# A conv, attention and scan kernel on one core: statistics of x through four 1 MB buffers, split arrival signals, and the second batch's first rows asked for slot by slot

## The chip, the cores and the metric

The kernel runs on one core of a Trainium2 chip. The metric is device time in microseconds (us), the median of several executions. Before the change it is 10475.02 us (three executions: 10473.13, 10475.02 and 10499.15).

## The reference, cut to what matters

```python
x = x + _L0_conv_ref(_gn(x), qkv_w, dw_w, proj_w, temperature)   # x: (2, 48, 512, 512) float32
x = x + _L1_conv_ref(_gn(x), down_w, down_b, right_w, right_b, left_w, left_b)

def _gn(v, G=16, eps=1e-5):            # group norm without scale and shift, 3 channels a group
    g = v.reshape(B_, G, C_ // G, H_, W_)
    m = jnp.mean(g, axis=(2, 3, 4), keepdims=True)
    s = jnp.var(g, axis=(2, 3, 4), keepdims=True)
    return ((g - m) / jnp.sqrt(s + eps)).reshape(v.shape)

def _L0_conv_ref(x, ...):
    qkv = conv_1x1(x, qkv_w)           # 48 -> 144 channels
    qkv = depthwise_3x3(qkv, dw_w)     # zero padding of one pixel
    q, k, v = split(qkv)               # each to (b, 8 heads, 6*16 rows, 128*128 tokens), 4x4 blocks
    q, k = q / norm(q), k / norm(k)
    attn = softmax(einsum('bhcn,bhdn->bhcd', q, k) * temperature)
    return conv_1x1(from_blocks(attn @ v), proj_w)
```

`_L1_conv_ref` runs four recurrent scans over the image (down, up, right, left), each step adding a five-tap convolution of the previous line. Only the first half of layer 0 is touched here: the group norm's mean and variance of x, and the fused 1x1 and 3x3 convolution that makes q, k and v.

## The kernel before, in words

**Stages.** `program` calls `attention`, `attention_weights_and_mix`, `scans` and `final_sum` one after the other. The change lies in `attention`, which takes the first 40% of the time. Each engine has its own instruction stream, written out by hand in the order in which it runs, and the streams meet only at semaphores.

**Statistics of batch 0.** x of batch 0 is 50.3 MB, seen as 128 partitions of 98304 numbers. SP loads it in `NCH` = 24 chunks of 2 MB (`CH` = 4096 numbers a partition) into the two slots of `xs` (`load_chunk`, L229). DVE runs eight BN_STATS of 512 numbers on each (`chunk_stats`, L528, L530), and its last one counts up `chunk_used[s]`, on which SP waits before it fills that slot again. The first two chunks are in flight before the constants and weights (`params`) are asked for; DVE then waits for `params`, multiplies the taps (L593, L595) and goes on with chunks 2 to 23. After the last chunk one aggregate (L543), two small reductions through TensorE and `row_stats` give mean and variance of every channel. Statistics of batch 1 are taken later, by small chunks, beside the convolution of batch 0; they are not touched.

**Convolution blocks.** A block is four image rows (`NT` = 128 blocks a batch). `raw` and `raw_edge` have two slots; block n lies in slot n % 2. `load_main` (L232) issues five DMAs: channels 0 to 31 in three row shifts and channels 32 to 47 in two. `load_edge` (L236) issues four: channels 32 to 47, the third row shift, in four column shifts. All nine count up one semaphore, `raw_in[b][s]`. ACT waits for all nine (`arrive`, L304), then makes `x_high` of x minus its mean (`high`, L297, k = 0 to 3, one a row) and `x_edge` (L300, k = 4 and 5). DVE makes the rounding remainder `x_low` (L629) and the lower half of `x_edge` (L633); its last one counts up `low_ready[b]`. That count tells PE that a block can be multiplied, and SP that its raw slot is free. PE computes four output rows a block (`row`, L430), each into one of two PSUM banks; ACT takes a row out (`take`, L334 and L335), DVE adds the other half to it (`add_up`, L644 and L645, signal `dve_moved`), and PE starts row dy only when row dy - 2 has been moved. ACT's order in a block is fixed: casts 0, 1, 2 of the next block, take 0, cast 3, square, cast 4, take 1, cast 5, the v copy, take 2, take 3.

**Borders.** Row -1 of the image is outside. `fill_top` (L610) writes the mean into row 0 of `raw` slot 0 and into the two border columns of `raw_edge`, of both slots at once, and signals `top_filled[b]`. `fill_end` (L619) does the same for the last row.

**The change of batch.** In before, SP loads blocks 0 and 1 of batch 1 when `top_filled[1]` has come. DVE runs `fill_top(1)` behind its `add_up` calls of block 126, after `low_ready[0]` = 128. ACT meets the wait for block 0 of batch 1 (`arrive(1, 0, 0)`) at the start of its block 127, ahead of its four takes of block 127. At the start of batch 0 SP asks for the main rows of blocks 0 and 1 early, and for the edge rows only after `top_filled[0]`.

Of the kernel before, what the change touches and what calls it, by code (L numbers as in the profile page):

```python
# [16 lines left out]
B, C, H, W = 2, 48, 512, 512  # L17
# [75 lines left out]
def attention(nc, sem, x, wqkv, dwqkv, gstat, gsel, g112, ident, weights, eye, g112_sb, sumsq, ones, gram_sb,  # L93
# [6 lines left out]
    EDGE = 64  # L100
    CH, FM = 4096, 512
    NCH = C * H * W // 128 // CH
# [10 lines left out]
    with ExitStack() as inner:  # L113
            def sbi(name, shape, dt=F32):
                return inner.enter_context(nc.sbuf_tensor(name, shape, dt))
# [9 lines left out]
            scan_taps = sbi("scan_taps", [PP, len(weights), 3, PP])  # L125
            xs = sbi("xs", [128, 2, CH])
            stats = sbi("stats", [128, NCH * PER, 6])
# [11 lines left out]
            vt = sbi("vt", [TOK, 2, HEADS, N * N, HC])  # L139
            v_out = xs[0:HD, 0, 0:2 * HEADS * (NB // 2) * TOK].rearrange("p (f h i t) -> p f h i t", f=2, h=HEADS, t=TOK)  # L140
            qk = xs[:, 1, 0:2 * HQ * HD].rearrange("p (s h n c) -> p s h n c", s=2, h=HQ, c=HC)
            xs1 = sbi("xs1", [128, 2, SMALL])
# [8 lines left out]
            cleared, params = sem("cleared"), sem("params")  # L151
            chunk = [sem("chunk0"), sem("chunk1")]
            chunk_used = [sem("chunk_used0"), sem("chunk_used1")]
            small = [sem("small_chunk0"), sem("small_chunk1")]
# [8 lines left out]
            def per_batch(name):  # L163
                return [sem(f"{name}_b{b}") for b in range(B)]

            raw_in = [[sem(f"qk_raw_in_b{b}_{s}") for s in range(2)] for b in range(B)]
            top_filled, end_filled = per_batch("top_filled"), per_batch("end_filled")
            high_ready, low_ready = per_batch("high_ready"), per_batch("low_ready")
# [3 lines left out]
            v_stored = [[sem(f"v_stored_b{b}_{s}") for s in range(2)] for b in range(B)]  # L172
            LOADS = 9

# [28 lines left out]
            with nc.Block() as block:  # L203
# [17 lines left out]
                def _(sp):  # L221
# [10 lines left out]
                    def load_main(b, n, s, top=False, end=False):  # L232
                        for at, ch, nch, shift in ((0, 0, 32, -1), (32, 0, 32, 0), (64, 0, 32, 1), (96, 32, 16, -1), (112, 32, 16, 0)):
                            to, frm = rows(n, shift, top, end)
                            sp.dma_start(raw[at:at + nch, s, to], x[b, ch:ch + nch, frm]).then_inc(raw_in[b][s], 16)
                    def load_edge(b, n, s, end=False):  # L236
                        to, frm = rows(n, 1, False, end)
                        for k in range(4):
                            a, e = max(0, 1 - k), min(W, W + 1 - k)
                            sp.dma_start(raw_edge[16 * k:16 * k + 16, s, to, a:e],  # L240
                                         x[b, 32:C, frm, a - 1 + k:e - 1 + k]).then_inc(raw_in[b][s], 16)

# [3 lines left out]

                    for s in range(2):
                        load_chunk(s, s)
# [10 lines left out]
                    for half in range(2):  # L259
                        for k in range(4):  # L260
                            at = 64 * half + 16 * k
                            sp.dma_start(w1[at:at + 16, 1], wqkv[32:C]).then_inc(params, 16)
                            for d in range(2):
                                if 0 <= d - k + 2 < 3:
                                    sp.dma_start(dwe[at:at + 16, d],
                                                 dwqkv[2, d - k + 2].unsqueeze(0).broadcast_to([16, QKV])).then_inc(params, 16)
                    with sp.Fori(1, NCH // 2) as i:
                        for s in range(2):

                            sp.wait_ge(chunk_used[s], i)  # L270
                            load_chunk(2 * i + s, s)
                    sp.wait_ge(tiles_clear, 1)
                    load_main(0, 0, 0, top=True)
                    load_main(0, 1, 1)
                    for b in range(B):
                        sp.wait_ge(top_filled[b], 1)
                        if b:
                            load(b, 0, 0, top=True)
                            load(b, 1, 1)
                        else:  # L280
                            load_edge(b, 0, 0)
                            load_edge(b, 1, 1)
                        with sp.Fori(1, NT // 2 - 1) as i:
                            for s in range(2):

                                sp.wait_ge(low_ready[b], 2 * i + s - 1)
                                load(b, 2 * i + s, s)
                        for s in range(2):
                            sp.wait_ge(low_ready[b], NT - 3 + s)
                            load(b, NT - 2 + s, s, end=s == 1)  # L290

                @block.scalar
                def _(act):
# [10 lines left out]
                    def arrive(b, n, s):  # L304

                        act.wait_ge(raw_in[b][s], 8 * LOADS * (n - s) + 16 * LOADS)

# [29 lines left out]
                    def group(b, g, first=False, last=False):  # L337
                        for i in range(NB):
                            n = NB * g + i
                            s = (i + 1) % 2  # L340
                            to_b, to_n = b, n + 1
                            if last and i == NB - 1:
                                to_b, to_n = b + 1, 0

                            def casts(*ks):
                                if to_b < B:
                                    for k in ks:
                                        high(to_b, to_n, s, k)

                            if to_b < B:  # L350
                                if last and i == NB - 2:
                                    act.wait_ge(end_filled[b], 1)
                                if last and i == NB - 1:
                                    act.wait_ge(negmean_ready, to_b + 1)

                                if not (first and i == 0):
                                    act.wait_ge(conv_done[b], N * n)
                                arrive(to_b, to_n, s)
                            casts(0, 1, 2)
                            if not (first and i < 2):  # L360

                                act.wait_ge(gram_done[b], n - 1)
                                act.wait_ge(vt_done[b], n - 1)
                            take(b, n, i, 0)
                            casts(3)
                            if not (first and i == 0):
                                square(b, n - 1, i - 1, first and i == 1)
                            casts(4)
                            take(b, n, i, 1)
                            casts(5)  # L370
                            if not (first and i == 0):
                                v_block(b, n - 1, g if i else g - 1, (i - 1) % NB)
                            take(b, n, i, 2)
                            take(b, n, i, 3)
# [18 lines left out]
                    arrive(0, 0, 0)  # L393
                    for k in range(CASTS):
                        high(0, 0, 0, k)
# [124 lines left out]
                def _(v):  # L520
# [66 lines left out]
                    nc.vector.memset(sumsq[:], 0.0).then_inc(sums_clear, 1)  # L587
                    for s in range(2):
                        v.wait_ge(chunk[s], 16)
                        chunk_stats(s, s)  # L590
# [5 lines left out]
                    link(ins)  # L596
                    with v.Fori(1, NCH // 2) as i:
                        for s in range(2):

                            v.wait_ge(chunk[s], 16 * i + 16)  # L600
                            chunk_stats(2 * i + s, s)
                    for s in range(2):
                        v.wait_ge(chunk_used[s], NCH // 2)
                    own_means()
# [4 lines left out]

                    def fill_top(b):  # L610

                        for a, e in ((0, 32), (96, 112)):
                            nc.vector.tensor_copy(raw[a:e, 0, 0], mean0[a:e, 0, b:b + 1].broadcast_to([e - a, W]))
                        for at in (0, W - 2):
                            ins = nc.vector.tensor_copy(raw_edge[:, :, :, at:at + 1].rearrange("p s r one -> p (s r one)"),
                                                        mean0[0:EDGE, 1, b:b + 1].broadcast_to([EDGE, 2 * N]))
                        ins.then_inc(top_filled[b], 1)

# [37 lines left out]
                    def group(b, g, first=False, last=False, sampled=False):  # L656
                        for i in range(NB):
# [23 lines left out]
                            if last and i == NB - 3:  # L681
                                v.wait_ge(low_ready[b], NT - 2)
                                fill_end(b)
                            if last and i == NB - 2 and b + 1 < B:
                                v.wait_ge(low_ready[b], NT)
                                fill_top(b + 1)

                    fill_top(0)
                    scaled_taps(0)
# [916 lines left out]
```

## Time and profile before

| What | Value |
|---|---|
| Median of three executions | 10475.02 us |
| Profiled execution: span, first to last instruction | 10449.6 us |
| Median less span (launch and end, outside the span) | 25.4 us |
| PE, DVE, ACT busy share of the span | 90%, 77%, 61% |
| Statistics of batch 0, chunks 2 to 23 | 32.44 to 167.65 us |
| First convolution of batch 0 | 191.39 us |
| PE's longest idle time between the batches | 10.07 us, until 2117.20 us |

The profile gives no time of its own for the profiled execution beyond its span, so a difference of spans is taken as a difference of times, with 25.4 us around the span. A timeline line has start, length, engine, line, operation and output <- inputs, with the count of merged instructions; the brackets at its end hold the idle time of the engine before it and what ended it. Starts are in us from the start of the span. SPq and ACTq lines are DMA issues.

### The profile page before, as it was taken

The page shows a single profiled execution, that of the slowest core. Times are in us where ns is not written, and L with a number is a line of the kernel's source. Part 1 is how long each engine was busy: PE and PEld are TensorE (multiplying, and loading weights), DVE is VectorE, ACT ScalarE, POOL GpSimd, SP SyncE. Part 2 cuts the span into 40 slices and gives each one's busy share as a digit, 9 for nine tenths or more (in the row PEclk, how much of TensorE's full clock was granted, in tenths as well). Part 3 has the DMA queues.
Part 4 walks back from the last instruction along what each step waited for, and adds up shares of the span by engine and source line. Part 5 has one row for each costly group of instructions (what it writes and reads, how often), then busy time and mean ns, then how long its engine had stood idle before and what let it go on. Part 6 is the DMA issues. An engine that isn't in the chain of part 4 may idle for free. (4 is left out here: it accounts for less than half of the span.)

```text
span 10449.6 us, 213663 instructions
## 1 busy us (share of the span) xinstructions
PE 9389.1 (90%) x72744; PEld 9047.4 (87%) x72744; DVE 8070.5 (77%) x16201; ACT 6339.0 (61%) x11047; POOL 2982.2 (29%) x4333
## 2 busy tenths in 40 slices
PE   2999999999999998999979999999999999999100
PEld 2999999999999998777779999999999999999100
DVE  7888888777777776998977777777799997777333
ACT  2777777767777775444456667999833336666100
POOL 0000000000000000000046666666666666666100
PEclk9999999999999998999989999999999999999555
DMA  8888887666666666999968887777766657777899
GB/s 246 166 167 164 167 166 144 125 125 130 133 129 133 132 131 127 270 266 256 267 156 198 199 202 185 211 217 214 208 209 213 220 194 190 198 197 204 346 431 406
DMA packets 740412, 2101.28 MB, mean 201 GB/s; under 512 B 58480, under 2 KB 633232, under 8 KB 649184
## 3 DMA queue, kind: packets, MB, share of 16 engines
q1 hardware_dynamic: 611920, 1744.17, 65.5%
q10 hardware_dynamic: 106368, 204.76, 6.1%
q0 software_dynamic: 22016, 151.01, 5.9%
q8 instruction: 55, 0.90, 0.0%
q14 instruction: 53, 0.43, 0.0%
HBM read 1344.51 MB, written 754.97 MB: 201 GB/s over the span
## 5 line engine op out<-in xcount | busy, mean ns | idle before, releaser
L1448 ACT CAST hi<-rough 112x256 fp32r<-112x256 f32 x4096 | 1666.8, 407 | 1410.8 <-DVE rough L1362 1359.8
L1282 PE MATMUL scan_ps<-hi,scan_high 112*112 112x256 f32 x12264 | 2125.0, 282 | 30.6 <-ACT hi L1448 30.6
L1362 DVE SCALAR_TENSOR_TENSOR rough<-scan_ps,scan_bias,lines 112x256 f32<-112x256 f32 x4086 | 2136.3, 523 | 19.0 <-issue 14.4
L1293 PE MATMUL scan_ps_low<-lo,scan_high 112*112 112x256 f32 x12264 | 2130.5, 282 | 1.1 <-POOL lo L1394 0.7
L1288 PE MATMUL scan_ps_low<-hi,scan_low 112*112 112x256 f32 x12264 | 2123.3, 281 | 0.0
L438 PE MATMUL conv_ps<-tap_high,x_high 128*128 128x432 f32 (+2 forms) x6144 | 1884.0, 307 | 27.6 <-DVE vt L645 15.7
L438 PE MATMUL conv_ps<-tap_low,x_high 128*128 128x432 f32 (+2 forms) x6144 | 1908.3, 311 | 0.0
L438 PE MATMUL conv_ps<-tap_high,x_low 128*128 128x432 f32 (+2 forms) x6144 | 1905.1, 310 | 0.0
L1282 PEld LDWEIGHTS scan_ps<-hi,scan_high 112*112 112x112 f32 x12264 | 1691.3, 175 | 32.1 <-ACT hi L1448 31.3
L1293 PEld LDWEIGHTS scan_ps_low<-lo,scan_high 112*112 112x112 f32 x12264 | 1684.7, 175 | 5.6 <-POOL lo L1394 2.8
L1288 PEld LDWEIGHTS scan_ps_low<-hi,scan_low 112*112 112x112 f32 x12264 | 1687.1, 176 | 0.0
L1394 POOL TENSOR_TENSOR lo<-lines,hi 112x256 fp32r<-112x256 f32 x2048 | 1414.5, 691 | 807.9 <-DVE lines L1367 786.2
L1394 POOL TENSOR_TENSOR lo<-ring,hi 112x256 fp32r<-112x256 f32 x2048 | 1414.0, 690 | 778.4 <-DVE ring L1367 776.7
L629 DVE SCALAR_TENSOR_TENSOR x_low<-raw,negmean,x_high 128x512 fp32r<-128x512 f32 x1024 | 1149.4, 1151 | 107.1 <-ACT x_high L297 107.1
L1367 DVE TENSOR_TENSOR ring<-scan_ps_low,rough 112x256 f32<-112x256 f32 x2044 | 868.8, 425 | 470.4 <-PE scan_ps_low L1293 436.3
L297 ACT ACTIVATE x_high<-raw,negmean 128x512 fp32r<-128x512 f32 x1024 | 1207.8, 1231 | 32.0 <-DMA raw_edge<-x 20.7
L438 PEld LDWEIGHTS conv_ps<-tap_high,x_high 128*128 128x128 f32 x6144 | 1162.1, 189 | 50.4 <-DVE vt L645 17.2
L438 PEld LDWEIGHTS conv_ps<-tap_high,x_low 128*128 128x128 f32 x6144 | 1166.4, 190 | 20.2
L438 PEld LDWEIGHTS conv_ps<-tap_low,x_high 128*128 128x128 f32 x6144 | 1162.5, 189 | 19.5 <-issue 0.2
L1367 DVE TENSOR_TENSOR lines<-scan_ps_low,rough 112x256 f32<-112x256 f32 x2044 | 867.6, 424 | 304.5 <-PE scan_ps_low L1293 222.0
L334 ACT COPY xs<-conv_ps 128x288 f32<-128x288 f32 x1024 | 408.9, 399 | 973.7 <-PE conv_ps L444 972.4
L644 DVE TENSOR_TENSOR xs<-conv_ps,xs 128x192 f32<-128x192 f32 x1024 | 365.2, 357 | 703.1 <-ACT vt L335 694.8
(140 smaller groups left out, 12398.8 us busy)
## 6 DMA issues: line engine op xcount, KB each, us to landing
raw<-x SPq DMA_DIRECT2D x764, 256.0 KB, 5.3
d_rows<-lines SPq DMA_DIRECT2D x32, 3584.0 KB, 30.2
u_cols<-lines SPq DMA_DIRECT2D x64, 1792.0 KB, 13.3
r_cols<-lines SPq DMA_DIRECT2D x32, 3584.0 KB, 24.3
lines<-u_cols SPq DMA_DIRECT2D x31, 3584.0 KB, 16.5
lines<-r_cols SPq DMA_DIRECT2D x30, 3584.0 KB, 16.6
lines<-d_rows SPq DMA_DIRECT2D x30, 3360.0 KB, 15.6
v_blocks<-xs ACTq DMA_DIRECT2D x128, 768.0 KB, 5.6
```

Source lines behind the costliest of these rows:

```text
L297: ins = nc.scalar.activation(x_high[:, s, k, :, 1:TOK + 1], phases(raw, s, k), ACT.Identity, bias=negmean0[:, 0, b:b + 1], scale=1.0)
L334: nc.scalar.copy(qk_at(i % 2, dy, 0, 3), qk_of(left))
L438: nc.tensor.matmul(bank(dy, side, lo - side, hi - side), xs[at], ws[taps], start=fresh[side], stop=False, skip_group_check=True)
L629: ins = nc.vector.scalar_tensor_tensor(x_low[:, s, k, :, 1:TOK + 1], phases(raw, s, k), negmean0[:, 0, b:b + 1], x_high[:, s, k, :, 1:TOK ...
L644: nc.vector.tensor_tensor(to(i % 2, dy, 1, 3), of(middle), to(i % 2, dy, 1, 3), ALU.add)
L1282: last = nc.tensor.matmul(ps[:, b, 0:LP], high[:, shift], hi[:, b, (k - 1) % 2, shift:shift + LP], start=shift == 0, stop=shift == 2)
L1288: nc.tensor.matmul(ps_low[:, b, 0:LP], low[:, shift], hi[:, b, (k - 1) % 2, shift:shift + LP], start=shift == 0, stop=False)
L1293: last = nc.tensor.matmul(ps_low[:, b, 0:LP], high[:, shift], lo[:, b, shift:shift + LP], start=False, stop=shift == 2)
L1362: nc.vector.scalar_tensor_tensor(rough[:, b, k % 2], ps[:, b, 0:LP], bias, line(way, s, k % T, b, kept), ALU.add, ALU.add).then_inc(rough_ ...
L1367: nc.vector.tensor_tensor(state(way, s, k, b), ps_low[:, b, 0:LP], rough[:, b, k % 2], ALU.add).then_inc(state_done[b], 1)
L1394: nc.gpsimd.tensor_tensor(lo[:, b, 1:LP + 1], state(way, k // T, k, b), hi[:, b, k % 2, 1:LP + 1], ALU.subtract).then_inc(lo_ready[b], 1)
L1448: nc.scalar.copy(hi[:, b, k % 2, 1:LP + 1], rough[:, b, k % 2]).then_inc(hi_ready[b], 1)
```

## The change

The chunk of the statistics becomes half as long and gets four slots instead of two; the loops on SP and DVE run over four slots. `v_out` and `qk`, which reuse the memory of `xs`, keep their addresses. The nine loads of a block count up two semaphores, `main_in` (5) and `edge_in` (4): `arrive` waits for the main rows alone, and ACT waits for the edge rows just ahead of cast 4. `fill_top` is called for each slot with a signal of its own. At the change of batch SP asks for the main rows of batch 1's block s as soon as `low_ready[0]` is 127 + s, and for its edge rows after `top_filled[1][s]`.

```diff
-    CH, FM = 4096, 512
+    CH, FM = 2048, 512
+    SLOTS = 4
...
-            xs = sbi("xs", [128, 2, CH])
+            xs = sbi("xs", [128, SLOTS, CH])
...
-                            sp.dma_start(raw[at:at + nch, s, to], x[b, ch:ch + nch, frm]).then_inc(raw_in[b][s], 16)
+                            sp.dma_start(raw[at:at + nch, s, to], x[b, ch:ch + nch, frm]).then_inc(main_in[b][s], 16)
...
-                                         x[b, 32:C, frm, a - 1 + k:e - 1 + k]).then_inc(raw_in[b][s], 16)
+                                         x[b, 32:C, frm, a - 1 + k:e - 1 + k]).then_inc(edge_in[b][s], 16)
...
-                    with sp.Fori(1, NCH // 2) as i:
-                        for s in range(2):
+                    with sp.Fori(1, NCH // SLOTS) as i:
+                        for s in range(SLOTS):
 
                             sp.wait_ge(chunk_used[s], i)
-                            load_chunk(2 * i + s, s)
+                            load_chunk(SLOTS * i + s, s)
                     sp.wait_ge(tiles_clear, 1)
                     load_main(0, 0, 0, top=True)
                     load_main(0, 1, 1)
                     for b in range(B):
-                        sp.wait_ge(top_filled[b], 1)
-                        if b:
-                            load(b, 0, 0, top=True)
-                            load(b, 1, 1)
-                        else:
-                            load_edge(b, 0, 0)
-                            load_edge(b, 1, 1)
+                        for s in range(2):
+                            if b:
+                                sp.wait_ge(low_ready[b - 1], NT - 1 + s)
+                                load_main(b, s, s, top=s == 0)
+                            sp.wait_ge(top_filled[b][s], 1)
+                            load_edge(b, s, s)
...
-                        act.wait_ge(raw_in[b][s], 8 * LOADS * (n - s) + 16 * LOADS)
+                        act.wait_ge(main_in[b][s], 8 * MAIN * (n - s) + 16 * MAIN)
+
+                    def edges_arrive(b, n, s):
+
+                        act.wait_ge(edge_in[b][s], 8 * EDGES * (n - s) + 16 * EDGES)
...
                                 if last and i == NB - 1:
                                     act.wait_ge(negmean_ready, to_b + 1)
+                                    act.wait_ge(top_filled[to_b][0], 1)
...
                                 square(b, n - 1, i - 1, first and i == 1)
+                            if to_b < B:
+                                edges_arrive(to_b, to_n, s)
                             casts(4)
...
                             if last and i == NB - 3:
                                 v.wait_ge(low_ready[b], NT - 2)
                                 fill_end(b)
+                                if b + 1 < B:
+                                    v.wait_ge(low_ready[b], NT - 1)
+                                    fill_top(b + 1, 0)
                             if last and i == NB - 2 and b + 1 < B:
                                 v.wait_ge(low_ready[b], NT)
-                                fill_top(b + 1)
+                                fill_top(b + 1, 1)
```

DVE's loop over the chunks and ACT's first block change in the same way: four slots in the one, and in the other casts 0 to 3 after the main rows and `top_filled[0][0]`, casts 4 and 5 after the edge rows.

SP's issues at the change of batch, before (`raw` is what `load_main` fills, `raw_edge` what `load_edge` fills):

```order
L240 DMA raw_edge<-x 16x3x510
L235 DMA raw<-x 32x1536 [waits top_filled_b1]
L235 DMA raw<-x 32x2048 x2
L235 DMA raw<-x 16x1536
L235 DMA raw<-x 16x2048
L240 DMA raw_edge<-x 16x4x511
L240 DMA raw_edge<-x 16x2048
```

The same place after:

```order
L242 DMA raw_edge<-x 16x3x510
L237 DMA raw<-x 32x1536 [waits low_ready_b0]
L237 DMA raw<-x 32x2048 x2
L237 DMA raw<-x 16x1536
L237 DMA raw<-x 16x2048
L242 DMA raw_edge<-x 16x4x511 [waits top_filled_b1_0]
L242 DMA raw_edge<-x 16x2048
L242 DMA raw_edge<-x 16x4x511
L242 DMA raw_edge<-x 16x4x510
L237 DMA raw<-x 32x2048 [waits low_ready_b0]
```

The five main DMAs of batch 1's block 0 hang on `low_ready` now, no longer on the filled border, and a wait stands ahead of its edge DMAs alone.

ACT's first block of batch 0, before:

```order
L297 ACTIVATE x_high<-raw,negmean0 128x4x128 [waits qk_raw_in_b0_0,negmean_ready,tiles_clear]
L297 ACTIVATE x_high<-raw,negmean0 128x4x128 x3
L300 ACTIVATE x_edge<-raw_edge,negmean0 64x512 x2
L297 ACTIVATE x_high<-raw,negmean0 128x4x128 [waits qk_raw_in_b0_1]
L297 ACTIVATE x_high<-raw,negmean0 128x4x128 x2
```

And after:

```order
L298 ACTIVATE x_high<-raw,negmean0 128x4x128 [waits raw_in_b0_0,top_filled_b0_0,negmean_ready,tiles_clear]
L298 ACTIVATE x_high<-raw,negmean0 128x4x128 x3
L301 ACTIVATE x_edge<-raw_edge,negmean0 64x512 [waits raw_edge_in_b0_0]
L301 ACTIVATE x_edge<-raw_edge,negmean0 64x512
L298 ACTIVATE x_high<-raw,negmean0 128x4x128 [waits raw_in_b0_1]
```

The wait for the edge rows has moved behind the four casts of the main rows.

## Rows read from the trace of the kernel before

**Rows 1.** Page: the span.
```profile
span 10449.6 us, 213663 instructions
```

**Rows 2.** Windows: busy us (count) of PE, PEld, DVE, ACT, POOL; clock, DMA, GB/s.
```profile
32.40:168.00 135.60, 0.00 (x0) 0.00 (x0) 106.80 (x177) 0.00 (x0) 0.00 (x0) 1.00 0.87 329
...
300.00:2000.00 1700.00, 1697.83 (x12693) 1670.08 (x12692) 1407.79 (x2802) 1269.08 (x1815) 48.02 (x91) 1.00 0.79 159
...
2000.00:2120.00 120.00, 109.61 (x805) 107.18 (x804) 85.61 (x180) 79.53 (x114) 0.00 (x0) 0.96 0.61 116
```

**Rows 3.** Waits from 0 to 320 us: total us, times, longest.
```profile
DVE stats L530 <- DMA xs<-x: 35.2, 23, 3.3
```

**Rows 4.** Timeline of DVE in the statistics.
```profile
32.44 4.84 DVE L530 BATCH_NORM_STATS2 stats<-xs 128x512 f32 x8 [3.26 <-DMA xs<-x]
...
37.59 4.85 DVE L530 BATCH_NORM_STATS2 stats<-xs 128x512 f32 x8 [0.31 <-DMA xs<-x]
...
45.58 9.72 DVE L530 BATCH_NORM_STATS2 stats<-xs 128x512 f32 x16 [3.15 <-DMA xs<-x]
...
107.61 4.84 DVE L530 BATCH_NORM_STATS2 stats<-xs 128x512 f32 x8 [2.31 <-DMA xs<-x]
...
162.81 4.84 DVE L530 BATCH_NORM_STATS2 stats<-xs 128x512 f32 x8 [0.93 <-DMA xs<-x]
```

**Rows 5.** DMA issues from 30 to 165 us: count, KB, us to landing.
```profile
xs<-x SPq DMA_DIRECT2D x20, 2048.0 KB, 7.2
```

**Rows 6.** Window in which both queued chunks are carried.
```profile
28.00:34.00 6.00, 0.00 (x0) 0.00 (x0) 2.74 (x8) 0.00 (x0) 0.00 (x0) 1.00 1.02 430
```

**Rows 7.** Timeline from the last statistics to the first matmul.
```profile
177.29 3.60 SPq L240 DMA_DIRECT2D raw_edge<-x  x8
...
180.08 0.45 DVE L574 TENSOR_TENSOR edge_low<-edge_f,edge_high 128x288 fp32r<-128x288 f32 x1
...
183.42 4.48 ACT L297 ACTIVATE x_high<-raw,negmean 128x512 fp32r<-128x512 f32 x4 [7.33 <-DMA raw_edge<-x]
...
187.81 2.29 ACT L300 ACTIVATE x_edge<-raw_edge,negmean 64x512 fp32r<-64x512 f32 x2
...
189.09 2.14 DVE L633 SCALAR_TENSOR_TENSOR x_edge<-raw_edge,negmean,x_edge 64x512 fp32r<-64x512 f32 x2
...
191.39 0.70 PE L438 MATMUL conv_ps<-tap_high,x_high 128*128 128x432 f32 x1 [11.96 <-DVE x_edge L633]
```

**Rows 8.** Timeline at the change of batch.
```profile
2078.44 2.19 DVE L633 SCALAR_TENSOR_TENSOR x_edge<-raw_edge,negmean,x_edge 64x512 fp32r<-64x512 f32 x2
...
2086.97 2.29 DVE L629 SCALAR_TENSOR_TENSOR x_low<-raw,negmean,x_high 128x512 fp32r<-128x512 f32 x2 [1.28 <-ACT x_high L297]
...
2098.55 0.41 ACT L334 COPY xs<-conv_ps 128x288 f32<-128x288 f32 x1 [1.54 <-PE conv_ps L444]
...
2100.74 0.24 DVE L615 COPY raw_edge<-mean 64x8 f32<-64x8 f32 x2
...
2101.01 2.17 SPq L235 DMA_DIRECT2D raw<-x  x5
...
2112.47 3.38 ACT L297 ACTIVATE x_high<-raw,negmean 128x512 fp32r<-128x512 f32 x3 [13.33 <-DMA raw_edge<-x]
...
2117.20 0.73 PE L438 MATMUL conv_ps<-tap_high,x_high 128*128 128x432 f32 x1 [10.07 <-DVE vt L645]
...
2125.66 0.40 ACT L334 COPY xs<-conv_ps 128x288 f32<-128x288 f32 x1 [2.62 <-PE conv_ps L444]
```

**Rows 9.** Page, DMA issues: count, KB, median us to landing.
```profile
raw<-x SPq DMA_DIRECT2D x764, 256.0 KB, 5.3
```

**Rows 10.** Window: the first conv row behind PE's idle time.
```profile
2117.20:2121.40 4.20, 4.20 (x16) 4.05 (x17) 4.20 (x6) 4.20 (x6) 0.00 (x0) 0.53 0.69 85
```

**Rows 11.** Timeline of ACT: take 1 of two usual blocks.
```profile
2031.47 0.41 ACT L334 COPY xs<-conv_ps 128x288 f32<-128x288 f32 x1 [0.58 <-PE conv_ps L444]
...
2046.43 0.40 ACT L334 COPY xs<-conv_ps 128x288 f32<-128x288 f32 x1 [0.56 <-PE conv_ps L444]
```

More of the change, by code:

```diff
@@ L139, in attention @@
             vt = sbi("vt", [TOK, 2, HEADS, N * N, HC])
-            v_out = xs[0:HD, 0, 0:2 * HEADS * (NB // 2) * TOK].rearrange("p (f h i t) -> p f h i t", f=2, h=HEADS, t=TOK)
-            qk = xs[:, 1, 0:2 * HQ * HD].rearrange("p (s h n c) -> p s h n c", s=2, h=HQ, c=HC)
+            v_out = flat(xs[0:HD])[:, 0:2 * HEADS * (NB // 2) * TOK].rearrange("p (f h i t) -> p f h i t", f=2, h=HEADS, t=TOK)
+            qk = flat(xs[:])[:, 2 * CH:2 * CH + 2 * HQ * HD].rearrange("p (s h n c) -> p s h n c", s=2, h=HQ, c=HC)
             xs1 = sbi("xs1", [128, 2, SMALL])
@@ L151, in attention @@
             cleared, params = sem("cleared"), sem("params")
-            chunk = [sem("chunk0"), sem("chunk1")]
-            chunk_used = [sem("chunk_used0"), sem("chunk_used1")]
+            chunk = [sem(f"chunk{s}") for s in range(SLOTS)]
+            chunk_used = [sem(f"chunk_used{s}") for s in range(SLOTS)]
             small = [sem("small_chunk0"), sem("small_chunk1")]
@@ L164, in per_batch @@
                 return [sem(f"{name}_b{b}") for b in range(B)]
-            raw_in = [[sem(f"qk_raw_in_b{b}_{s}") for s in range(2)] for b in range(B)]
-            top_filled, end_filled = per_batch("top_filled"), per_batch("end_filled")
+            main_in = [[sem(f"raw_in_b{b}_{s}") for s in range(2)] for b in range(B)]
+            edge_in = [[sem(f"raw_edge_in_b{b}_{s}") for s in range(2)] for b in range(B)]
+            top_filled, end_filled = [[sem(f"top_filled_b{b}_{s}") for s in range(2)] for b in range(B)], per_batch("end_filled")
             high_ready, low_ready = per_batch("high_ready"), per_batch("low_ready")
@@ L172, in attention @@
             v_stored = [[sem(f"v_stored_b{b}_{s}") for s in range(2)] for b in range(B)]
-            LOADS = 9
+            MAIN, EDGES = 5, 4
             def bank(dy, side, lo, hi):
@@ L266, in _ @@
                                                  dwqkv[2, d - k + 2].unsqueeze(0).broadcast_to([16, QKV])).then_inc(params, 16)
-                    with sp.Fori(1, NCH // 2) as i:
-                        for s in range(2):
+                    with sp.Fori(1, NCH // SLOTS) as i:
+                        for s in range(SLOTS):
                             sp.wait_ge(chunk_used[s], i)
-                            load_chunk(2 * i + s, s)
+                            load_chunk(SLOTS * i + s, s)
                     sp.wait_ge(tiles_clear, 1)
@@ L393, in _ @@
                     arrive(0, 0, 0)
-                    for k in range(CASTS):
+                    act.wait_ge(top_filled[0][0], 1)
+                    for k in range(N):
+                        high(0, 0, 0, k)
+                    edges_arrive(0, 0, 0)
+                    for k in range(N, CASTS):
                         high(0, 0, 0, k)
@@ L587, in _ @@
                     nc.vector.memset(sumsq[:], 0.0).then_inc(sums_clear, 1)
-                    for s in range(2):
+                    for s in range(SLOTS):
                         v.wait_ge(chunk[s], 16)
@@ L596, in _ @@
                     link(ins)
-                    with v.Fori(1, NCH // 2) as i:
-                        for s in range(2):
+                    with v.Fori(1, NCH // SLOTS) as i:
+                        for s in range(SLOTS):
                             v.wait_ge(chunk[s], 16 * i + 16)
-                            chunk_stats(2 * i + s, s)
-                    for s in range(2):
-                        v.wait_ge(chunk_used[s], NCH // 2)
+                            chunk_stats(SLOTS * i + s, s)
+                    for s in range(SLOTS):
+                        v.wait_ge(chunk_used[s], NCH // SLOTS)
                     own_means()
@@ L608, in _, with fill_top @@
                     v.wait_ge(tiles_clear, 1)
-                    def fill_top(b):
-                        for a, e in ((0, 32), (96, 112)):
-                            nc.vector.tensor_copy(raw[a:e, 0, 0], mean0[a:e, 0, b:b + 1].broadcast_to([e - a, W]))
+                    def fill_top(b, s):
+                        if s == 0:
+                            for a, e in ((0, 32), (96, 112)):
+                                nc.vector.tensor_copy(raw[a:e, 0, 0], mean0[a:e, 0, b:b + 1].broadcast_to([e - a, W]))
                         for at in (0, W - 2):
-                            ins = nc.vector.tensor_copy(raw_edge[:, :, :, at:at + 1].rearrange("p s r one -> p (s r one)"),
-                                                        mean0[0:EDGE, 1, b:b + 1].broadcast_to([EDGE, 2 * N]))
-                        ins.then_inc(top_filled[b], 1)
+                            ins = nc.vector.tensor_copy(raw_edge[:, s, :, at:at + 1].rearrange("p r one -> p (r one)"),
+                                                        mean0[0:EDGE, 1, b:b + 1].broadcast_to([EDGE, N]))
+                        ins.then_inc(top_filled[b][s], 1)
                     def fill_end(b):
@@ L683, in group @@
                                 fill_end(b)
+                                if b + 1 < B:
+                                    v.wait_ge(low_ready[b], NT - 1)
+                                    fill_top(b + 1, 0)
                             if last and i == NB - 2 and b + 1 < B:
                                 v.wait_ge(low_ready[b], NT)
-                                fill_top(b + 1)
-                    fill_top(0)
+                                fill_top(b + 1, 1)
+                    for s in range(2):
+                        fill_top(0, s)
                     scaled_taps(0)
```

## The prediction

> **What bounds the kernel now.** I read the page first: the span is 10449.6 us [rows 1], and the last chain runs through stages that the change doesn't touch, so what is gained in the attention stage shifts everything behind it. Next came the windows. In the convolution of batch 0 PE is busy 1697.8 of 1700 us [rows 2]: nothing that spares ACT or DVE a wait there can pay. Two stretches are different. In the statistics (32.4 to 168 us) PE does nothing, DVE is busy 106.8 of 135.6 us and the DMA engines 0.87 at 329 GB/s: neither is full [rows 2]. Around the change of batch PE is idle for about 10 us of 120 [rows 2]. The waits and the timelines then say what is waited for: chunks of x, 35.2 us in 23 waits [rows 3], and once at the start of each batch the edge rows, 7.33 and 13.33 us on ACT [rows 7, 8].
>
> **Term 1, statistics.** Now two slots of 2 MB alternate. DVE needs 4.84 us for eight BN_STATS (9.72 for sixteen in a row, so a change of chunk costs almost nothing) [rows 4]; a chunk takes 7.2 us from issue to landing [rows 5]; a slot's cycle is 4.84 + 7.2 + about 0.3 for signals = 12.3 us for two chunks, 6.15 a chunk. Twenty-two chunks give 135.3 us; the trace has 32.44 to 162.81 + 4.84 = 167.65, which is 135.2 [rows 4]. So it is latency that bounds, not rate.
>
> How fast does x come when a second chunk is already queued? The loop's first two chunks were: the second could start 37.59 - 32.44 = 5.15 us after the first, with DVE waiting 0.31 us for it [rows 4]. So 2 MB cost 5.15 us in a queue, against 7.2 alone, and some 2.1 us of the latency overlaps. While both are carried the engines move 430 GB/s, 4.88 us for 2 MB [rows 6]. Half a chunk then costs 2.42 us on DVE and 2.44 to 2.58 us on the DMA side. A 1 MB slot's cycle is 2.42 + 0.3 + (7.2 - 2.5) = 7.4 us, and four slots have 4 x 2.5 = 10 us for it: the queue never runs dry. I take 2.5 us a chunk, between DVE's rate and the queued DMA's. The loop's first 1 MB lands half a chunk (about 2.45 us) before 32.44, so at 30.0; two more issues ahead of the weights may delay those by up to 0.9 us, of which I take 0.4. The end is 30.4 + 43 x 2.5 + 2.42 = 140.3 us, not 167.65: **27 us gained**. Bounds: at DVE's pace 30.0 + 44 x 2.42 = 136.5, 31 us gained; at 2.58 us a chunk with the whole delay 144.3, 23 us gained. What no row shows is 1 MB pieces in this pattern, 8 KB a partition where now it is 16. Its lower bound is no gain at all, if half the bytes take half of today's pace, 3.07 us; the nearest row (two queued chunks) speaks for the upper part.
>
> The Trainium skill, "DMA: Bandwidth & Descriptors", section Bandwidth, lists 341 GB/s for one transfer of 1 MB and 425 for 16 MB; by the first a chunk would take 3.07 us, the loop 135.3 us, and this term would be nothing. The queued pair and the 430 GB/s window of this trace [rows 4, 6] stand against it, though both are of 2 MB pieces. The same section gives about 358 GB/s as what one core gets from memory; by that figure the loop's 46.1 MB need 129 us and the term is 6 us, but the trace exceeds it already.
>
> **Term 2, first block of batch 0.** The border is filled and SP issues the edge DMAs from 177.29; ACT starts at 183.42, when slot 0's have landed, and the main rows lie there long before [rows 7]. After, ACT casts rows 0 to 3 from 177.3 to 181.8 (4.48 us) and the edges from 183.4 to 185.7 (2.29 us) [rows 7]. DVE ends the scaled taps at 180.53, does four `x_low` at 1.1 us each to about 185.1, then the two edge parts in 2.14 us to 187.3, where now it ends at 189.09 + 2.14 = 191.23 [rows 7]. PE starts at 187.5, not 191.39: **4 us gained**. What is late next is DVE, not a load. Bounds 3 and 5 us. The four small copies in place of two cost DVE about 0.3 us, inside its wait.
>
> **Term 3, change of batch.** The remaining lows of block 126 end at 2078.44 + 2.19 = 2080.63 [rows 8]; that is `low_ready` = 127, so the main rows of batch 1's block 0 are issued then and not at 2101.01 [rows 8]. Five issues take 2.2 us [rows 8] and landing 5.3 [rows 9]: there by 2089. `fill_top(1, 0)` runs behind `fill_end`, ahead of the low at 2086.97. Its copies (0.84 + 0.24 us) fit the 1.28 us that DVE waits there [rows 8]. The four edge DMAs go out at 2087 and, with some 7 us as at the start, are there by 2096. ACT comes to its casts at 2098.55 + 0.6 = 2099.1 [rows 8] and waits for nothing, where now it waits 13.33 us [rows 8]. Behind those casts stand ACT's takes of block 127, which free the PSUM banks for which PE waits 10.07 us [rows 8]. PE's first row behind it runs at a granted clock of 0.53, near the lower level of 1.2 GHz, after those 10 us idle [rows 10]; that goes too. The whole of it shows in take 3 of block 127: it comes 2125.66 - 2098.55 = 27.11 us after that of block 126 [rows 8], where a usual block takes 2046.43 - 2031.47 = 14.96 us [rows 11]. **12 us gained**; bounds 10 (PE's wait alone) and 13.3 (ACT's whole wait). What is late next is the store of v and the 7 us behind it, which shift as they are.
>
> **What it adds.** Each block gets one more wait on ACT, ahead of cast 4, with a register operation in the loops. Behind it stand cast 4 and take 1, for which DVE and PE wait. In a usual block ACT waits 0.56 to 0.58 us for PE ahead of take 1 [rows 11], so an added 0.05 to 0.1 us lies in that gap: 0. Without the cover, 254 blocks at 0.1 us would be 25 us. The edge rows are asked for a block earlier and are there. The doubled number of chunk issues on SP (0.33 us each in 2.5) is no bound. PE's stream is the same.
>
> **Sum.** 27 + 4 + 12 = 43 us off the profiled execution: span 10449.6 to 10407. That execution's time outside its span is taken as the 25.4 us by which the median exceeds it, so the forecast is 10475 - 43 = **10432 us**, 0.41% less. A measurement of this kernel tells about 0.3%, 31 us, from no change: below 10444 counts as faster.
>
> **Rivals.**
> - A: the chunks keep today's pace, 3.07 us a MB, since smaller pieces don't stream at the queued pair's rate. For it: no row shows 1 MB pieces; DMA share 0.87 [rows 2] looks near full. Against: the queued pair's 5.15 us and 430 GB/s. The terms left are 4 + 12 = 16: 10459 us, no change. The row for 1 MB in the Trainium skill ("DMA: Bandwidth & Descriptors", Bandwidth) would give this case.
> - B: the wait at the change of batch moves, not goes: ACT stops for something else ahead of the takes (the early main rows behind other traffic, or the border of slot 0, late because its low is late). For: nothing in the rows is that late, the margin is 3 us at the edge rows. Against: 10 us of margin for the main rows. Term 3 gone, 31 left: 10444 us, on the boundary.
> - C, slower: transfers of one queue don't overlap their fixed part. A 1 MB chunk would then need 7.2 - 2.5 = 4.7 us, whatever is queued, 44 of them 207 us against 135: 72 us lost, 16 won, 10531 us. The case is worse than before from 3.07 + 16/44 = 3.43 us a chunk. Against it speaks again the pair 5.15 us apart where one alone takes 7.2.
>
> **Chances.** Forecast 0.77, its own range 10424 to 10442; A and what lies between (2.7 to 3.07 us a chunk) 0.13; B 0.06; C 0.04. Faster than by 0.3%: 0.77 + 0.03 from B = 0.80; within: 0.13 + 0.03 = 0.16; slower: 0.04. The range goes from 10423 (all terms at their upper bounds, 31 + 5 + 13 = 49 us, with 3 us for spread between runs) to 10455, which leaves out C and the full form of A.
>
> **What would show it.** Statistics ending near 140 us, DVE's waits there under 10 us in all, chunks every 2.4 to 2.6 us; spacings of 3 us mean A, 4.7 mean C. The first matmul of the convolution 4 us closer to the last statistics (19.7 us behind it now 23.7). At the change of batch no wait of ACT for `raw_edge`, no 10 us gap of PE, and take 3 of block 127 near 15 us behind that of 126. PE idle for more than 3 us in a middle window of 1700 us would make my zero for the added waits wrong.

## The result, and the profile after

The changed kernel takes 10425.74 us (median of 10 executions, 10405.43 to 10445.3) against 10474.69 us (10 executions, 10449.32 to 10499.15). The medians are 49 us apart. The ratio with its 95% interval, 0.9959 (0.9949 to 0.9969), stands for 43 us (32 to 53). The forecast was 43 us less and a time of 10432 us. Two later timings on other occasions, told below, gave 0.9977 for the same kernel and 0.999 for the kernel before against itself, whose two medians were 15.5 us apart all the same (10459.18 and 10474.72), so the total is known less well than one interval says. The profiled span falls by only 15.6 us, from 10449.6 to 10434.0, where the forecast had 10407. One execution of the kernel before, on a later occasion, took 18417.67 us at a granted clock of 0.551, where all others show 0.955 to 0.958; it is in none of the ratios. Where the time went is read from the traces.

Statistics, timeline of DVE after; answers to [rows 4]:

```profile
29.83 106.88 DVE L542 BATCH_NORM_STATS2 stats<-xs 128x512 f32 x172 [1.01 <-DMA xs<-x]
138.38 2.47 DVE L542 BATCH_NORM_STATS2 stats<-xs 128x512 f32 x4 [1.66 <-DMA xs<-x]
140.98 5.36 DVE L555 BATCH_NORM_AGGREGATE mv<-stats 128x2 f32<-128x1152 f32 x1
```

Its wait for chunks from 0 to 320 us (total, times, longest) and the DMA queue from 30 to 130 us, answers to [rows 3, 5]:

```profile
DVE stats L542 <- DMA xs<-x: 3.4, 4, 1.7
```

```profile
DMA packets 5777, 42.03 MB, mean 420 GB/s; under 512 B 647, under 2 KB 647, under 8 KB 647
...
xs<-x SPq DMA_DIRECT2D x40, 1024.0 KB, 7.1
```

The last statistics end at 140.85 us, not 167.65. DVE is fed without a wait for 172 instructions, which are 43 pieces in 106.88 us, 2.49 us each. A 1 MB chunk now takes 7.1 us to land, as much as 2 MB did: it stands in a queue, and that costs nothing.

First block of batch 0, timelines of SP, ACT and PE; answers to [rows 7]:

```profile
150.50 4.18 SPq L242 DMA_DIRECT2D raw_edge<-x  x8
...
150.59 4.52 ACT L298 ACTIVATE x_high<-raw,negmean 128x512 fp32r<-128x512 f32 x4 [1.28 <-DVE raw_edge L628]
156.62 2.29 ACT L301 ACTIVATE x_edge<-raw_edge,negmean 64x512 fp32r<-64x512 f32 x2 [1.51 <-DMA raw_edge<-x]
...
160.31 0.70 PE L450 MATMUL conv_ps<-tap_high,x_high 128*128 128x432 f32 x1 [7.34 <-DVE x_edge L646]
```

ACT casts while the edge rows travel; 1.51 us of waiting remain of 7.33. From the last statistics to the first matmul are 19.46 us, before 23.74.

Change of batch, timelines of DVE, SP and ACT; answers to [rows 8]:

```profile
2046.68 2.19 DVE L646 SCALAR_TENSOR_TENSOR x_edge<-raw_edge,negmean,x_edge 64x512 fp32r<-64x512 f32 x2
...
2048.90 2.18 SPq L237 DMA_DIRECT2D raw<-x  x5
...
2054.70 0.24 DVE L628 COPY raw_edge<-mean 64x4 f32<-64x4 f32 x2
...
2054.96 1.73 SPq L242 DMA_DIRECT2D raw_edge<-x  x4
...
2066.79 0.41 ACT L339 COPY xs<-conv_ps 128x288 f32<-128x288 f32 x1 [1.52 <-PE conv_ps L456]
2067.26 3.45 ACT L298 ACTIVATE x_high<-raw,negmean 128x512 fp32r<-128x512 f32 x3
...
2081.80 0.40 ACT L339 COPY xs<-conv_ps 128x288 f32<-128x288 f32 x1 [2.63 <-PE conv_ps L456]
```

The main rows go out when the low of block 126 is done, the edge rows when the border is filled, and the cast at 2067.26 has no wait. Take 3 of block 127 comes 15.01 us after that of block 126; before it was 27.11 [rows 8].

In between nothing changed; window of the changed kernel, columns as in [rows 2]:

```profile
300.00:1969.00 1669.00, 1666.81 (x12457) 1639.54 (x12455) 1380.71 (x2748) 1246.33 (x1780) 47.17 (x89) 1.00 0.78 159
```

PE idles 2.2 us in 1669, as before in 1700. The added wait in each block is hidden.

### The profile page after: what moved, and what is told of

Its sections match the earlier page's. It is cut to its first block and busy times, and to the rows that moved or that the text cites. A ratio compares the mean times of both kernels' runs of the same rounds, so it can differ in the third digit from the quotient of the medians.

```text
span 10434.0 us, 213912 instructions
## 1 busy us (share of the span) xinstructions
PE 9405.2 (90%) x72744; PEld 9056.3 (87%) x72744; DVE 8073.5 (77%) x16205; ACT 6337.2 (61%) x11047; POOL 2991.9 (29%) x4333
```

## The experiments

Four landmarks were read from every profile, in us: the start of the aggregate behind the statistics (end of statistics), the first conv matmul, the start of the last transposes of v (end of the attention stage), and the length of the mixing stage, from its first matmul to the first matmul of the scans.

| Kernel | Statistics end | First conv | Last v transposes | Mixing stage | Span |
|---|---|---|---|---|---|
| before | 167.8 | 191.4 | 4056.6 | 1207.7 | 10449.6 |
| before_again | 168.2 | 191.7 | 4052.8 | 1218.1 | 10454.0 |
| before_third | 168.0 | 191.6 | 4054.6 | 1221.7 | 10458.8 |
| after | 141.0 | 160.3 | 4009.2 | 1229.7 | 10434.0 |
| after_again | 141.3 | 160.6 | 4008.1 | 1234.7 | 10434.9 |
| stats_only | 141.6 | 165.1 | 4028.9 | 1231.9 | 10460.5 |
| signals_only | 168.3 | 187.7 | 4034.8 | 1222.5 | 10455.5 |
| handover_only | 168.8 | 192.1 | 4039.8 | 1234.8 | 10461.2 |
| split_only | 168.0 | 187.3 | 4047.5 | 1235.7 | 10462.2 |
| two_of_1mb | 198.7 | 218.0 | 4066.4 | 1212.5 | 10471.4 |
| three_of_1mb | 142.6 | 162.3 | 4009.3 | 1225.3 | 10425.1 |
| six_of_half_mb | 144.3 | 163.6 | 4011.9 | 1237.2 | 10435.2 |
| half_the_stats | 141.7 | 161.1 | 4010.1 | 1220.7 | 10424.2 |
| store_wait_later | 141.3 | 160.7 | 4006.5 | 1225.3 | 10421.2 |

### One part at a time

**stats_only**, on the kernel before:

```diff
-    CH, FM = 4096, 512
+    CH, FM = 2048, 512
+    SLOTS = 4
...
```

> The kernel before with the statistics of x through four 1 MB buffers alone; signals and the change of batch as before. Theory (three independent terms, 27 + 4 + 12 us): statistics end at 140 to 142 us as in the changed kernel, the last transposes of v in the attention stage (4056.6 us before, 4009.2 after) near 4029, total about 27 us less (10448 us). Rival (the early signals need the faster statistics, or the terms overlap): statistics end the same, but the last transposes come near 4020 or 4040.

Measured: ratio 0.9975 (0.9960 to 0.9989), which is 26 us (12 to 42). Last transposes at 4028.9, 25.8 us ahead of the mean of the three profiles of before, 4054.7. Those three spread over 3.8 us, so a distance at this landmark is good to some 2 us.

**signals_only**, on the changed kernel:

```diff
-    CH, FM = 2048, 512
-    SLOTS = 4
+    CH, FM = 4096, 512
+    SLOTS = 2
...
```

> The changed kernel with the old statistics (two buffers of 2 MB): split signals and slot-by-slot loads at the change of batch alone. Theory: statistics end at 167.6 us as before, first convolution 4 us sooner, 12 to 16 us less at the change of batch, last transposes of v near 4037, total 16 to 20 us less (10457 us). Rival (split signals cost ACT something in each of 254 blocks): last transposes near 4045 or later.

Measured: last transposes at 4034.8, 19.9 us ahead, a little better than expected. 25.8 + 19.9 = 45.7, and the whole change has 46.0 (4054.7 less 4008.7, the mean of its two profiles): at this landmark the parts add up. The totals do not: the ratio is 0.9968 (0.9956 to 0.9980), 33 us (21 to 46) where 16 to 20 were expected, and 26 + 33 = 59 us is more than the whole change gave in either timing (43 and 24 us).

**handover_only**, on the kernel before (signals of the nine loads not split; `fill_top` slot by slot as in the change):

```diff
...
-                        sp.wait_ge(top_filled[b], 1)
+                        for s in range(2):
+                            if b:
+                                sp.wait_ge(low_ready[b - 1], NT - 1 + s)
+                                load_main(b, s, s, top=s == 0)
+                            sp.wait_ge(top_filled[b][s], 1)
+                            load_edge(b, s, s)
...
```

> The kernel before with the slot-by-slot loads at the change of batch alone; one signal for all nine loads, old statistics. Theory (at the change of batch the early issue does it all, since the edge rows too are there in time): no wait of ACT at the change of batch, 12 to 16 us gained there, first block as before (ACT waits 7.3 us), last transposes of v near 4042. Rival (the split is needed there too): ACT still waits some us for edge rows, last transposes near 4048.

Measured: last transposes 14.9 us ahead of before. ACT at the change of batch:

```profile
2099.66 3.46 ACT L296 ACTIVATE x_high<-raw,negmean 128x512 fp32r<-128x512 f32 x3
```

The cast follows with no wait: there the split gives nothing.

**split_only**, signals_only with the loads at the change of batch asked for as before (DVE fills the borders of both slots behind block 126 again):

```diff
...
-                                sp.wait_ge(low_ready[b - 1], NT - 1 + s)
-                                load_main(b, s, s, top=s == 0)
-                            sp.wait_ge(top_filled[b][s], 1)
-                            load_edge(b, s, s)
+                            sp.wait_ge(top_filled[b][s], 1)
+                        for s in range(2):
+                            if b:
+                                load_main(b, s, s, top=s == 0)
+                            load_edge(b, s, s)
...
```

> The changed kernel with split signals alone: old statistics, and at the change of batch all loads are asked for only after both borders are filled, as before. Theory: first block 4 us sooner; at the change of batch ACT starts when the main rows have landed, near 4 us sooner than with all nine loads, so its wait falls from 13.3 to about 9 us; last transposes of v near 4048. Rival (split gives all of the gain at the change of batch): ACT's wait there is gone, last transposes near 4040.

Measured: last transposes 7.2 us ahead, some 4.3 of them at the first block, and ACT's wait at the change of batch:

```profile
2104.73 3.39 ACT L298 ACTIVATE x_high<-raw,negmean 128x512 fp32r<-128x512 f32 x3 [9.90 <-DMA raw<-x]
```

The wait is 9.90 us instead of 13.33, and now for main rows. Both expectations held.

### What sets the pace of the statistics

These four start from the changed kernel. **two_of_1mb** (the memory of `xs` stays as large):

```diff
-    SLOTS = 4
+    SLOTS = 2
...
```

> The changed kernel with only two of its four 1 MB buffers in use. Theory (latency: issue to landing of 1 MB is 4.7 us, of which 2.3 don't shrink with the size; slot cycle 2.45 + 0.3 + 4.7 = 7.4 us for two pieces): 3.7 us a piece, statistics end near 192 us. Rival (the gain comes from smaller pieces, not from more in flight): statistics end near 141 us or at most at 168.

Measured: statistics end at 198.7 us, 7 us later than expected. Two slots of 1 MB lose 31 us against two of 2 MB, so smaller pieces by themselves are not the gain. Its DMA issues from 32 to 130 us, and the beginning and end of one slot's cycle on DVE:

```profile
xs<-x SPq DMA_DIRECT2D x26, 1024.0 KB, 4.8
```

```profile
124.32 2.47 DVE L542 BATCH_NORM_STATS2 stats<-xs 128x512 f32 x4 [2.05 <-DMA xs<-x]
...
131.90 2.47 DVE L542 BATCH_NORM_STATS2 stats<-xs 128x512 f32 x4 [2.12 <-DMA xs<-x]
```

A slot's cycle is 131.90 - 124.32 = 7.58 us for two pieces, 3.79 each. 1 MB takes 4.8 us to land where 2 MB took 7.2 [rows 5]: by these two rows 2.4 us a MB and 2.4 us that don't shrink.

**three_of_1mb** (SLOTS = 3):

> The changed kernel with three of its four 1 MB buffers in use. Theory: slot cycle 7.4 us against 3 x 2.45 = 7.35 us of work, so just enough: statistics end at 141 to 146 us. Rival (four are needed, because a queued piece takes longer to land than one alone): 150 us or more.

Measured: 142.6 us, 1.6 us later than with four. The cycle of 7.58 us over the loads' 2.49 us a piece (below) is 3.0 slots, and three are nearly enough; the theory held.

**six_of_half_mb** (SLOTS = 6, CH = 1024):

> The changed kernel with six buffers of 0.5 MB for the statistics. Theory (with enough in flight the size of a piece does not matter, DVE's rate bounds): slot cycle 1.2 + 0.3 + 3.5 = 5 us against 6 x 1.24 = 7.4: statistics end at 140 to 142 us. Rival (a price for each piece, on the DMA side or in semaphores): 0.1 us or more a piece of 96 pieces, end at 150 us or later.

Measured: 144.3 us, between theory and rival: 3.3 us more than with four of 1 MB, which is 0.07 us for each of the 48 pieces that there are more. The core's DMA engines moved 409 GB/s from 32 to 130 us, with four of 1 MB 420; whether that or something on DVE makes the price was not separated.

**half_the_stats** (BN_STATS on every second 512 numbers):

```diff
-                        for k in range(PER):
+                        for k in range(0, PER, 2):
...
```

> The changed kernel that leaves out every second BN_STATS of the statistics of batch 0, so its means and variances are not those of x. All loads are as they were; it shows the rate of the loads alone. Theory (DVE and DMA are nearly balanced; DMA gives 430 GB/s, 2.44 us a MB): statistics end near 138 us, DVE now waiting for every piece. Rival (DMA has much in reserve, DVE alone bounds): end at 125 us or sooner.

Measured: 141.7 us, 3.7 us later than the theory had it and no sooner than with all the work. DVE's timeline:

```profile
127.34 1.29 DVE L542 BATCH_NORM_STATS2 stats<-xs 128x512 f32 x2 [1.18 <-DMA xs<-x]
...
132.31 1.29 DVE L542 BATCH_NORM_STATS2 stats<-xs 128x512 f32 x2 [1.18 <-DMA xs<-x]
```

With DVE idle half of the time the chunks still come 2.49 us apart (two spacings are 132.31 - 127.34 us), 1.049 MB / 2.49 us = 421 GB/s. The loads set the pace, and DVE, which needs 9.72 / 4 = 2.43 us a piece [rows 4], just keeps up. By this run a faster DVE would gain nothing here.

### The stages behind

> The changed kernel once more, unaltered. Theory (the attention stage is the same from run to run, the stages behind it scatter by some 20 us): last transposes of v at 4009 within 2 us, its distance to the end of the span anywhere from 6390 to 6430 us. Rival (the change costs 30 us in the stages behind): that distance is again near 6425 us, where before it was 6393, and the total ratio is nearer to 0.998.

Measured: ratio 0.9977 (0.9966 to 0.9988), 24 us (13 to 36). Last transposes at 4008.1, as the theory said; the rest of the span 6426.8 us, 6424.8 in the first profile of after and 6393.0 in that of before, as the rival said.

> The kernel before once more, unaltered, timed against itself. Theory (the stage that mixes the values scatters from execution to execution, whatever the attention stage did): last transposes of v at 4056.6 within 2 us, and the stage from there to the first scan matmul longer than in the first profile of before (1207.7 us from its first matmul), somewhere up to 1237 as in the other kernels' profiles; ratio to itself within 0.998 to 1.002. Rival (an attention stage that is over sooner makes the mixing stage 15 to 25 us longer): the mixing stage is again at 1205 to 1212 us.

> The same kernel for one more profile. Theory: its mixing stage differs by 5 us or more from one of the other two profiles of this kernel. Rival: all three lie within 5 us around 1208 us.

Measured: ratio of the kernel to itself 0.999 (0.998 to 1.000), as expected. Last transposes at 4052.8, 3.8 us before the first profile, where 2 us were allowed: a miss. The mixing stage takes 1218.1 and 1221.7 us, after 1207.7 in the first profile. So the first profile of before was one of the shorter ones, and the rival falls in the form in which it was put. But all three lie below both of after (1229.7 and 1234.7). The other nine kernels, none of which touches that stage, range from 1212.5 to 1237.2.

The same holds of the whole rest of the span, from the last transposes to its end: 6393.0, 6401.2 and 6404.2 us in the three profiles of before, 6424.8 and 6426.8 in the two of after, 6405.0 to 6431.6 in the nine others. The means of before and after differ by 26 us, 16 of them in the mixing stage and 10 in the scans. In the mixing stage the difference goes with DVE's wait for the loads of x there (`res`): 21.9, 42.9 and 42.6 us in the three profiles of before, 49.9 and 54.7 in the two of after, 31.7 in two_of_1mb, whose stage is the shortest of the nine (1212.5), and 56.6 in six_of_half_mb, whose stage is the longest (1237.2). Why those loads come later is not known. Nor is it shown that the change does it: there are few profiles, and single executions differ by as much. The first profiled execution of before, if it too lasted 1.6 us more than its span, was 23 us shorter than its median, and that of before_again 4 us shorter; that of after was 10 us longer, that of after_again 5 us shorter. The attention stage gave 46 us and the two timings 43 and 24, which leaves 3 and 22 us lost behind it, each with an interval of some 10 us to either side. These runs leave open how much of that is a cost of the change.

### A version that goes further

**store_wait_later**, on the changed kernel:

```diff
-                            for s in range(2):
-                                act.wait_ge(v_stored[b - 1][s], 16 * G)
...
+                        if i % 2 == 0 and isinstance(g, int) and g == 0 and b:
+                            act.wait_ge(v_stored[b - 1][half], 16 * G)
```

> The changed kernel, but at the start of batch 1 ACT does not wait for the last two stores of v; the wait stands ahead of the first copy into each half of v_out instead. Theory (the next thing late at the change of batch is that store: ACT waits 6.4 us for it, PE 2.2 us and then a row at half clock): ACT starts 6 us sooner, last transposes of v 4 to 7 us before 4009, total 4 to 7 us less, which is below what the times can tell. Rival (the casts of block 1 were hidden beside PE's reset and first rows anyway): under 2 us.

Measured: last transposes at 4006.5, 1.6 us ahead of after_again (2.7 of the first profile of after), so the expectation missed and its rival held. ACT at the start of batch 1 in it:

```profile
2088.82 3.48 ACT L298 ACTIVATE x_high<-raw,negmean 128x512 fp32r<-128x512 f32 x3 [0.71 <-ACT xs L322]
2093.94 0.41 ACT L341 COPY xs<-conv_ps 128x288 f32<-128x288 f32 x1 [1.64 <-PE conv_ps L456]
```

In after_again ACT waited 5.77 us for the stores and PE 1.59 us ahead of the third row of batch 1's first block. Here ACT's wait is gone, but its next take then waits for PE: only the 1.6 us that PE had waited there could be won. The time, 10416.6 us (5 executions) with a ratio of 0.9958 (0.9945 to 0.9972) to before, is the best median of that occasion, 25 us below that of after_again (10441.87). 1.6 us explain no more of it. In the profiles the rest of the span is 12 us shorter (6414.7 against 6426.8), which by the section above no edit of the attention stage is known to cause. It is no proof of a faster kernel beyond the 1.6 us.

## Why the prediction was right, point by point

- **Statistics, 27 us.** 26.8 in the trace (167.65 to 140.85); in stats_only the statistics end 26.4 us sooner and the last transposes come 25.8 us sooner. The mechanism, latency with too little in flight, is shown by two_of_1mb (too few, slower than before) and three_of_1mb. What I left between two bounds, 2.5 us a chunk, is the loads' rate of 2.49 us. Rival A (3.07 us) and C (4.7 us) are ruled out. The Trainium skill ("DMA: Bandwidth & Descriptors", Bandwidth) has 341 GB/s for one transfer of 1 MB; queued ones ran at 421 GB/s here, so its figure does not carry over to them. The same section of the Trainium skill has about 358 GB/s for each of the two cores of a pair when both stream; here one ran.
- **First block, 4 us.** 4.3 (23.74 to 19.46 us from the last statistics to the first matmul). DVE is late next, as said: PE still waits for its `x_edge`.
- **Change of batch, 12 us.** 12.1 (27.11 to 15.01). Handover_only shows that the early issue makes it; the split is worth 3.4 us of ACT's wait there only if the issue stays late. Rival B is ruled out: the cast has no wait. A little more came behind it, mis-sized as "shift as they are": 46.0 us in the attention stage against 43.2 for the three terms (26.8 + 4.3 + 12.1). Of these 2.8 us, 2.0 lie between take 3 of block 127 and take 3 of batch 1's first block: 26.38, 23.62 and 25.82 us in the three profiles of before, 24.39 and 22.22 in the two of after, so the gain is no larger than the spread of one kernel. In this stretch PE has a second idle time. Before, it is 3.10 us, and the row behind it runs at a low clock (0.54 in the window's third column from the right):

```profile
2142.72 0.73 PE L438 MATMUL conv_ps<-tap_high,x_high 128*128 128x432 f32 x1 [3.10 <-DVE vt L645]
...
2142.70:2149.00 6.30, 6.28 (x24) 6.09 (x25) 4.94 (x8) 3.13 (x6) 0.00 (x0) 0.54 0.06 12
```

After:

```profile
2097.93 0.46 PE L450 MATMUL conv_ps<-tap_high,x_high 128*128 128x432 f32 x1 [2.16 <-DVE vt L658]
```

The clock there is what varies between executions of one kernel: in before 0.54, 0.70 and 1.00 behind 3.10, 2.51 and 1.89 us of idle time, in after 0.60 and 1.00 behind 2.16 and 1.59 us.
- **Added waits, 0.** PE's idle time in the middle window (2.2 us in 1669) and the sum of the parts at the last transposes leave no room for a price in the attention stage.
- **The total.** The attention stage gives 46 us (47.4 in the first pair of profiles). The first timing gave 43 us, the second 24. That the first agrees with the forecast is in part luck, because one step of the prediction was not borne out: that what is gained in the attention stage shifts everything behind it. The profiled span came to 10434.0 and not 10407, with the rest of the span 6424.8 us after 6393.0; over all profiles of both kernels it is 26 us longer behind the change. As told above, part of this is scatter, and the cause is open. A second step was wrong: I took the span and the median to differ by 25.4 us of launch and end. Every later execution lists time and span 1.5 to 1.9 us apart (10435.59 and 10434.0), so the profiled execution of before, with its span of 10449.6, was most likely one of its shorter ones. The forecast of the time didn't suffer, since it used the median and a difference.

## What to carry to other kernels

When neither the engine nor the DMA engines are full and a two-slot ring alternates, compare issue to landing with the spacing of two transfers that were queued together: the difference is what more in flight can hide, and the slots needed are the cycle of one slot over the pace (here 7.58 / 2.49, and three were nearly enough). Where one signal covers loads of unequal lateness, first see whether they can be asked for sooner; here splitting the signal paid only where they could not. A gain in one stage is a gain in the whole only if the stages behind keep their length, and that has to be measured too. A gain of 0.4% is better proved by a landmark inside the trace than by total times that scatter by as much.

## What the runs showed of the hardware that was not expected

Loads of x from HBM ran at 422 GB/s from 32 to 130 us with DVE half idle (half_the_stats), and at 277 GB/s in a ring of two 1 MB slots (two_of_1mb), where a transfer took 2.4 us beyond its 2.4 us a MB. Three executions of the kernel before differed by 14 us in the mixing stage (1207.7 to 1221.7), with DVE's wait for loads there between 21.9 and 42.9 us, while the end of their statistics agreed within 0.5 us. The row behind PE's second idle time, in batch 1, ran at a granted clock of 0.54, 0.70 and 1.00 in these three.
